# Flamingo-style four-layer block: the causal attention of the second layer in two halves of the tokens, the first one beside the gather

## The chip, the cores and the metric

The kernel runs on one core of a Trainium2 chip. A core has TensorE (PE, with its weight loads as PEld), VectorE (DVE), ScalarE (ACT), GpSimd (POOL) and SyncE (SP), and 16 DMA engines. The metric is device time in microseconds, median of the runs; the time before is 6575.31 us (three runs, 6571.84 to 6575.43).

## The reference

There are 2048 tokens of width 256 and a context of M = 1601 rows. Each of four layers (0 to 3) adds a gated attention to x and then a gated feed-forward. What matters here is this order and layer 2's attention:

```python
x = x + tanh(g_xattn[0]) * _L0_xattn_ref(ctx, ctx, layernorm(x), ...)   # sampled: 80 gathered rows a token
x = x + tanh(g_ffn[0])   * _L0_ffn_ref(layernorm(x), ...)               # with a convolution over tokens, width 3
x = x + tanh(g_xattn[1]) * _L1_xattn_ref(layernorm(x), ctx, ctx, ...)   # all 1601 keys
x = x + tanh(g_ffn[1])   * _L1_ffn_ref(layernorm(x), ...)
x = x + tanh(g_xattn[2]) * _L2_xattn_ref(layernorm(x), ctx, ctx, ...)   # causal
x = x + tanh(g_ffn[2])   * _L2_ffn_ref(layernorm(x), ...)               # experts, over all tokens
...
# _L2_xattn_ref: 16 heads of 16
q, k, v = query @ Wq.T, key @ Wk.T, value @ Wv.T
causal = arange(sq)[:, None] >= arange(sk)[None, :]     # token i sees context rows 0..i, of the 1601
out = softmax(where(causal, q k^T * SCALE, NEG)) v;  out @ Wo.T
```

A token of layers 1 and 2 needs nothing of the tokens after it, and of the tokens before it only what the convolution of layer 0 takes from its neighbour.

## The kernel before, in words

**Tokens and stages.** Tokens are in NT = 16 tiles of 128. `ALL_STAGES` places stages one after the other. Between two stages every engine that takes part waits for the others to be done (`run`). A stage placed with `skip=("pool",)` and others "beside" it lets POOL work on its own stage while PE, ACT, DVE and SP go through the stages beside.

**The gather.** `stage_gather_late` is POOL's: for each of the 7 last token tiles it issues 80 indirect DMAs (`gather`, L1319), each of which brings one row a partition from a table in memory to `got_late`, and then stores the tile (2.56 MB) to `late_rows` (L1391). Beside it stand three stages for tokens 0 to 1023: the convolution feed-forward of layer 0, the attention of layer 1 and the gated feed-forward of layer 1. `stage_sample_late` comes after both and loads `late_rows` (L1412, first loads L1224 and L1225); it computes the layer 0 attention of the last 7 tiles. Then come the same three stages for tokens 1024 to 2047, then the attention of layer 2 for all tokens, then the experts.

**An attention stage** (`stage_attention(env, keep, scratch, n, t0, nt)`, tokens of tiles t0 to t0+nt):

- Start: layer norm, the query projection in float32, split into bfloat16 parts and stored to `q_parts` (24 DMAs, L372).
- Heads in 8 pairs; hh is 0 or 1 in a pair. For each head there are two passes over the scores. The maximum pass ("max") multiplies queries by keys with tokens as rows (L657, causal diagonal L660) and reduces on DVE (L789); its "row" step (L795, L797) makes the negated maxima, which SP stores and loads back as one more row of `q_exp` (L877, L879). The exponential pass ("score") multiplies with keys as rows (L675, diagonal L678), ACT takes exp (L745), and the "sum" step multiplies the result by the values in float32 (L694), four groups of T/4 tokens side by side on the array. DVE copies the sums out at the end of a head (L802), SP stores them in 8 DMAs (`store_sums`, L885 and L887).
- The order is written out ahead: `exp_timeline` and `max_timeline` give each step a due time from costs, and the sorted list is the order in which PE, and with it DVE, work. `max_only` holds the maxima of the first pair, `both` is the loop's body (the exponential steps of a pair and maxima of the next, 7 times), `exp_last` the last pair. ROW_LEAD = 12 puts the maxima of a head 12 us ahead of its exponentials.
- SP's loop is, for each pair and each hh: `load_exp` (L868, L869: waits until the scores of the same hh of the pair before are through), `load_row` (L877 four times, waits for the row and for the store, then L879), `load_max` of the next pair (L861, L862), `store_sums` of the pair before (waits for the store at its end).
- End: the denominators go through memory (L917 to L940), DVE multiplies by their inverse (L814), PE projects (L721), DVE adds to X (L832).

For layer 2 a query tile t sees min(1601, 128(t+1)) keys, a key tile t is seen from token 128t on.

Of the kernel before, what the change touches and what calls it, by code (L numbers as in the profile page):

```python
# [16 lines left out]
P = 128  # L17
S = 2048
D = 256
DC = D // P  # L20
NT = S // P
# [4 lines left out]
M = 1601  # L26
MT = (M + P - 1) // P
# [458 lines left out]
def stage_attention(env, keep, scratch, n, t0, nt):  # L486
# [10 lines left out]
    tag = f"a{n}_{t0}"  # L497
    own = n == 3
    causal = n == 2
    keys = M + S if own else M  # L500
    KT = MT + (NT if own else 0)
    PE_CH, PE_SUM, ACT_FIXED, ACT_CH = 0.22, 0.92, 0.5, 0.37
    ROW_LEAD = 12.0
    SUM_LAG = 1.0
# [3 lines left out]
    def sb(name, shape, dt=f32, where=scratch):  # L508
        return where.enter_context(nc.sbuf_tensor(f"{tag}_{name}", shape, dt))

    def sem(name):
        return env.sem(f"{tag}_{name}")


    tiles = [(P * t, min(P, M - P * t), P * t if causal else 0, causal) for t in range(MT)]
    if own:
        tiles += [(M + P * t, P, P * t, True) for t in range(NT)]

# [1 line left out]
    exp_units = []  # L520
    order = [(hh, t) for hh in range(2) for t in range(KT)]
    for hh, t in order:
        for c in range(tiles[t][2] // CH, chunks):
            exp_units.append((hh, t, c, max(tiles[t][2], CH * c)))
    unit_of = {(hh, t, c): i for i, (hh, t, c, _) in enumerate(exp_units)}
    last_chunk_tile = {c: max(t for t in range(KT) if tiles[t][2] < SUM * (c + 1)) for c in range(4)}

    max_units, max_steps = [], []
    for hh in range(2):
        for t in range(nt):  # L530
            seen = M + P * (t + 1) if own else (min(M, P * (t + 1)) if causal else M)
            d0 = M + P * t if own else P * t
            d1 = min(d0 + P, seen) if (own or causal) else d0
            for k0 in range(0, seen, MAX_COLS):
                max_steps.append(("max", len(max_units)))
                max_units.append((hh, t, k0, min(MAX_COLS, seen - k0), d0, d1))
        max_steps.append(("row", hh))
# [3 lines left out]
    def exp_timeline(hh):  # L541


        out, now = [], 0.0
        for t in range(KT):
            units = [i for i, u in enumerate(exp_units) if u[0:2] == (hh, t)]
# [32 lines left out]
    wq, wo = sb("wq", [P, DC, D]), sb("wo", [P, DC, D])  # L579
    values = sb("values", [P, KT, D])  # L580
    q_bias = sb("q_bias", [P, DC])
# [13 lines left out]
    probs = [sb(f"probs{k}", [P, CH]) for k in range(PROB_SLOTS)]  # L595
    v_head = [sb(f"v_head{k}", [P, KT, 32]) for k in range(2)]
    sums = [sb(f"sums{k}", [P, SUM]) for k in range(2)]
# [8 lines left out]
    w_in, qb_ready, self_v, self_out = sem("w_in"), sem("qb_ready"), sem("self_v"), sem("self_out")  # L606
# [144 lines left out]
    def vector(dve):  # L751
# [31 lines left out]
        def steps(x, what, last=False):  # L783
            for s in what:
# [13 lines left out]
                elif s[0] == "out":  # L798
                    hh = s[1]
                    dve.wait_ge(sums_done, x * NS_ + (KT * (hh + 1) + NS_))  # L800
                    dve.wait_ge(sums_free, x * 2 + hh + 1)
# [36 lines left out]
    def sync(sp):  # L838
# [6 lines left out]
        if own:  # L845
            sp.dma_start(wk[:, :, :], dram["wk3"].rearrange("(c p) e -> p c e", p=P)).then_inc(w_in, 16)
            sp.dma_start(wv[:, :, :], dram["wv3"].rearrange("(c p) e -> p c e", p=P)).then_inc(w_in, 16)
        sp.dma_start(values[:, 0:MT, :], env.v_rows[n]).then_inc(w_in, 16)
        if n == 1:
            any_masked = sp.value_load(mask["flag"][0:1, 0:1])  # L850
            with sp.If(any_masked > 0):
# [472 lines left out]
def sample_buffers(env, keep):  # L1324

    def sb(name, shape, dt=env.f32):
        return keep.enter_context(env.nc.sbuf_tensor(name, shape, dt))
    env.Q0, env.frac, env.rows = sb("queries", [P, NT, D]), sb("frac", [P, NT, NO]), sb("rows", [P, NT + 1, NO], env.i32)
    env.got_late = sb("got_late", [P, NO, 4 * HD])
    env.numbers = sb("numbers", [P, NO], env.i32)  # L1330
# [834 lines left out]
def build(nc, dram):  # L2165
# [3 lines left out]
    with ExitStack() as keep:  # L2169
# [15 lines left out]
        def place(make, *args, hold=None, skip=(), beside=()):  # L2185
# [3 lines left out]
            with ExitStack() as scratch:  # L2189
# [4 lines left out]
                append(emitters, (), own)  # L2194

        ALL_STAGES(env, place, keep)
        block = keep.enter_context(nc.Block())

# [40 lines left out]
def ALL_STAGES(env, place, keep):  # L2239
    from contextlib import ExitStack  # L2240
    half = NT // 2
    place(stage_prep)
    env.any_masked = keep.enter_context(env.nc.sbuf_tensor("any_masked", [1, 1], env.i32))
    with ExitStack() as sampling:
        sample_buffers(env, sampling)
        with ExitStack() as front:
            place(stage_ctx, hold=front)
            place(stage_sample_points, hold=front)
            place(stage_sample_early, skip=("pool",), beside=(
                (stage_kv, (1,), True), (stage_quant,), (stage_fill,), (stage_mask_flag,),  # L2250
                (stage_sample_first,), (stage_kv, (2, 3), False)))
        place(stage_gather_late, skip=("pool",), beside=(
            (stage_conv_ffn, 0, half), (stage_attention, 1, 0, half), (stage_gated_ffn, 0, half)))
        place(stage_sample_late)
    place(stage_conv_ffn, half, half)
    place(stage_attention, 1, half, half)
    place(stage_gated_ffn, half, half)
    place(stage_attention, 2, 0, NT)
    place(stage_expert_ffn, 2)
    place(stage_attention, 3, 0, NT)  # L2260
    place(stage_expert_ffn, 3)
    place(stage_store)
# [68 lines left out]
```

## Time and profile before

| | us |
|---|---|
| median of 3 runs | 6575.31 |
| lowest, highest | 6571.84, 6575.43 |
| span of the profiled execution | 5943.9 |
| PE busy (of the span) | 3795.9 (64%) |
| DVE busy | 2791.6 (47%) |
| ACT busy | 1990.8 (33%) |
| POOL busy | 1506.2 (25%) |
| mean granted TensorE clock | 0.791 |
| layer 2 attention, from L839 to the last L832 | 2834.2 to 3488.2 |

The span runs from the first to the last instruction of one profiled execution; the page gives no time of that execution from outside, and the median lies 631.4 us over the span. Busy times are sums over the whole span; the stages have different limits, so a change in one stage is read from that stage. The granted clock is 1.00 at 2.4 GHz and 0.50 at 1.2 GHz.

### The profile page before, as it was taken

To read this page: it belongs to the slowest core of one execution; us is meant where nothing else is said; L and a number is where in the kernel's file an instruction comes from. 1 tells how busy PE (TensorE), PEld (TensorE's weight loads), DVE (VectorE), ACT (ScalarE), POOL (GpSimd) and SP (SyncE) were. 2 spreads that over 40 slices of the span, in tenths; PEclk is the share of its full clock that TensorE was granted. 3 is DMA by queue.
4 is the path that set the end of the run, shared out by engine and by line. 5 is a ranking of instruction groups with operands and counts; after the bars stand their busy time and mean duration, and the time that the engine had idled before them with its cause. 6 is when DMAs were issued, how large, how long until landed. Compare 5 with 4: busy or idle time off the path is not lost.

```text
span 5943.9 us, 71309 instructions
## 1 busy us (share of the span) xinstructions
PE 3795.9 (64%) x19888; PEld 1731.9 (29%) x19894; DVE 2791.6 (47%) x3817; ACT 1990.8 (33%) x3720; POOL 1506.2 (25%) x1461
## 2 busy tenths in 40 slices
PE   7700410037962013996599969974899999997695
PEld 2300200022321001332133336862222222222485
DVE  3131221276753276776566630013766666673201
ACT  1100100014751001673155621212366666664131
POOL 0767777677767400000000010010000000000202
PEclk9555655557986555998699979986799999999698
DMA  2331311013321211110211111534100111101243
GB/s 83 90 118 24 108 38 24 21 55 106 92 93 39 92 66 48 51 51 20 81 52 47 42 60 65 192 137 117 43 25 25 32 33 33 33 25 32 110 181 135
DMA packets 195461, 403.88 MB, mean 68 GB/s; under 512 B 46405, under 2 KB 130649, under 8 KB 186074
## 3 DMA queue, kind: packets, MB, share of 16 engines
q1 hardware_dynamic: 147114, 323.79, 17.0%
q0 software_dynamic: 48112, 77.16, 4.6%
q8 instruction: 122, 2.00, 0.1%
q14 instruction: 113, 0.93, 0.1%
HBM read 301.77 MB, written 106.10 MB: 69 GB/s over the span
## 4 chain that ended last, share of the span: by engine, by line
PE 47%; POOL 20%; DVE 10%; issue 10%; DMA 7%; ACT 2%; SPq 1%; POOLq 1%; DVEq 1%; ACTq 0%; PEldq 0%
POOL got_late L1319 13%; PE PS L694 13%; PE PS L657 9%; PE PS L675 8%; POOL s_got L1319 6%; PE PS L1959 5%; PE PS L1969 5%; DVE a_maxima L789 3%; ACT a_probs L745 1%; DMA q_parts<-a_parts 1%; PE PS L1929 1%; DMA late_rows<-got_late 1%; PE PS L1937 1%; PE PS L1122 1%; DMA Y<-denominators 1%
## 5 line engine op out<-in xcount | busy, mean ns | idle before, releaser
L789 DVE TENSOR_REDUCE a_maxima<-PS 128x1 f32<-128x1024 f32 (+8 forms) x1696 | 1637.9, 990 | 685.3 <-PE PS L657 468.7
L745 ACT ACTIVATE a_probs<-PS 128x512 f32<-128x512 f32 (+4 forms) x2896 | 1503.3, 572 | 771.7 <-PE PS L675 568.3
L657 PE MATMUL PS<-a_k_max,a_q_max 96*128 96x512 bf16 (+2 forms) x3136 | 913.5, 371 | 153.1 <-DVE a_maxima L789 90.4
L675 PE MATMUL PS<-a_q_exp,a_k_exp 97*128 97x512 bf16 (+4 forms) x2896 | 970.2, 376 | 58.6 <-ACT a_probs L745 30.6
L694 PE MATMUL PS<-a_probs,a_v_head 128*32 128x256 f32 (+4 forms) x7456 | 964.5, 496 | 31.8 <-DVE a_v_head L804 11.2
L2145 POOL IOTA e_slot_no<- 128x23 f32 x2 | 0.3, 162 | 2944.1 <-DVEq L2207 2944.1
L1319 POOL DMA_INDIRECT got_late<-kv_table,numbers x560 | 576.8, 1030 | 171.9 <-issue 171.9
L675 PEld LDWEIGHTS PS<-a_q_exp,a_k_exp 97*128 97x128 bf16 (+1 forms) x2896 | 271.7, 99 | 697.6 <-ACT a_probs L745 442.7
L657 PEld LDWEIGHTS PS<-a_k_max,a_q_max 96*128 96x128 bf16 x3136 | 263.8, 100 | 692.9 <-DVE a_maxima L789 386.6
L1319 POOL DMA_INDIRECT s_got<-kv_table,s_numbers x400 | 428.5, 1071 | 121.9 <-issue 121.9
L1298 PE MATMUL PS<-identity,s_ctx 128*128 128x128 f32 x18 | 6.2, 449 | 668.9 <-DVE s_ctx L1274 668.9
L1319 POOL DMA_INDIRECT got_late<-kv_table,s_numbers x320 | 348.5, 1089 | 96.9 <-issue 96.9
L1959 PE MATMUL PS<-e_slotT,e_w 128*128 128x256 f32 x1280 | 287.2, 383 | 11.7 <-DMA e_w<-in_ew 11.7
L2011 ACT ACTIVATE e_hid<-PS,e_w 128x256 f32<-128x256 f32 x320 | 151.4, 473 | 409.2 <-PE PS L1959 409.2
L694 PEld LDWEIGHTS PS<-a_probs,a_v_head 128*32 128x32 f32 (+1 forms) x7456 | 169.3, 108 | 407.9 <-ACT a_probs L745 241.8
L1969 PE MATMUL PS<-e_w,e_hid 128*128 128x256 f32 x1280 | 283.0, 379 | 1.4 <-ACT e_hid L2011 1.4
L1959 PEld LDWEIGHTS PS<-e_slotT,e_w 128*128 128x128 f32 x1280 | 246.1, 192 | 46.4 <-issue 12.3
L1969 PEld LDWEIGHTS PS<-e_w,e_hid 128*128 128x128 f32 x1280 | 240.2, 190 | 33.1 <-issue 2.2
L2158 POOL DMA_INDIRECT e_got<-slots_out,e_place_i x64 | 64.0, 999 | 711.3 <-SPq L1893 692.4
L1287 ACT ACTIVATE s_weight<-s_score 128x80 f32<-128x80 f32 x9 | 2.4, 269 | 634.9 <-DVE s_score L1266 634.9
L1298 PE MATMUL PS<-identity,m_ctx 128*128 128x128 f32 x14 | 4.8, 447 | 326.4 <-DVE m_ctx L1274 326.4
L1298 PEld LDWEIGHTS PS<-identity,s_ctx 128*128 128x128 f32 x18 | 2.6, 204 | 674.4 <-DVE s_ctx L1274 674.4
(342 smaller groups left out, 3309.9 us busy)
## 6 DMA issues: line engine op xcount, KB each, us to landing
e_w<-in_ew SPq DMA_DIRECT2D x41, 2052.0 KB, 8.1
late_rows<-got_late POOLq DMA_DIRECT2D x7, 2560.0 KB, 7.9
m_got<-late_rows SPq DMA_DIRECT2D x7, 2560.0 KB, 9.2
a_k_max<-k_parts SPq DMA_DIRECT2D x48, 300.2 KB, 3.8
a_k_exp<-k_parts SPq DMA_DIRECT2D x48, 300.2 KB
a_q_max<-q_parts SPq DMA_DIRECT2D x32, 384.0 KB, 3.6
a_q_exp<-q_parts SPq DMA_DIRECT2D x32, 384.0 KB
a_k_max<-k_parts SPq DMA_DIRECT2D x16, 684.2 KB, 5.7
```

The source lines that it names most:

```text
L657: last = pe.matmul(bank[:, b0:b1], q_max[hh][:, P * t:P * (t + 1)], k_max[hh][:, k0 + b0:k0 + b1], start=True, stop=not (lo < hi or masked))
L675: last = pe.matmul(bank[0:rows, q - CH * c:CH], k_exp[hh][:, k0:k0 + rows], q_exp[hh][:, q:CH * (c + 1)], start=True, stop=not (on_diag or ...
L694: last = pe.matmul(sum_bank[32 * c:32 * c + 32, q - SUM * c:SUM], v_head[hh][0:rows, t, :], probs[i % PROB_SLOTS][0:rows, q - at:SUM * (c ...
L745: act.activation(probs[i % PROB_SLOTS][0:rows, q - CH * c:CH], exp_bank[i % EXP_BANKS][0:rows, q - CH * c:CH], ACT.Exp).then_inc(probs_rea ...
L789: dve.tensor_reduce(maxima[hh][:, t, k0 // MAX_COLS:k0 // MAX_COLS + 1], max_bank[s[1] % MAX_SLOTS][:, 0:w], AX.X, ALU.max).then_inc(max_t ...
L1122: pe.matmul(bank, env.CT[:, c, c0:c0 + P], wkv[:, c, :], start=(c == 0), stop=False)
L1319: pool.indirect_dma_start(out=got[:, j, :], out_offset=None, in_=env.table, in_offset=bass.IndirectOffsetOnAxis(ap=numbers[:, j:j + 1].bit ...
L1929: last = pe.matmul(PS[:, f % 4, :], w1[1][:, c, P * f:P * (f + 1)], env.YT[:, c, CH * chunk:CH * (chunk + 1)], start=(c == 0), stop=(c == ...
L1959: last = pe.matmul(PS[:, f % 4, 0:SLOT], w1[k][:, c, P * f:P * (f + 1)], slotT[k][:, c, :], start=(c == 0), stop=(c == DC - 1))
L1969: last = pe.matmul(PS[:, 4 + k, D * j:D * (j + 1)], hid[k][:, f, P * j:P * (j + 1)], w2[k][:, f, :], start=(f == 0), stop=(f == FT - 1))
L2011: act.activation(hid[k][:, f, 0:SLOT], PS[:, f % 4, 0:SLOT], ACT.Gelu_apprx_tanh, bias=b1[k][:, f:f + 1]).then_inc(hid_out, 1)
L2158: pool.indirect_dma_start(out=got[t % FETCH][:, k, :], out_offset=None, in_=env.slots_out, in_offset=bass.IndirectOffsetOnAxis(ap=place_i[ ...
```

## The change

The causal attention takes a first token tile t0 that is not 0 and a number of tiles that is not 16, and it is placed twice: tiles 0 to 7 as a fourth stage beside the gather, tiles 8 to 15 where the whole was. Key tiles are cut to those that the half can see (`CT`: 8 of 13 for the first half, 13 for the second); in the second half the key tiles below t0 are seen by all of its tokens and have no diagonal. The value rows that are loaded are cut in the same way.

```diff
@@ stage_attention
-    keys = M + S if own else M
-    KT = MT + (NT if own else 0)
+    keys = M + S if own else (min(M, P * (t0 + nt)) if causal else M)
+    CT = (keys + P - 1) // P if causal else MT
+    KT = CT + (NT if own else 0)
...
-    tiles = [(P * t, min(P, M - P * t), P * t if causal else 0, causal) for t in range(MT)]
+    tiles = [(P * t, min(P, M - P * t), max(0, P * (t - t0)) if causal else 0, causal and t >= t0) for t in range(CT)]
...
-            seen = M + P * (t + 1) if own else (min(M, P * (t + 1)) if causal else M)
-            d0 = M + P * t if own else P * t
+            seen = M + P * (t + 1) if own else (min(M, P * (t0 + t + 1)) if causal else M)
+            d0 = M + P * t if own else P * (t0 + t)
...
-        sp.dma_start(values[:, 0:MT, :], env.v_rows[n]).then_inc(w_in, 16)
+        sp.dma_start(values[:, 0:CT, :], env.v_rows[n][:, 0:CT, :]).then_inc(w_in, 16)
@@ ALL_STAGES
         place(stage_gather_late, skip=("pool",), beside=(
-            (stage_conv_ffn, 0, half), (stage_attention, 1, 0, half), (stage_gated_ffn, 0, half)))
+            (stage_conv_ffn, 0, half), (stage_attention, 1, 0, half), (stage_gated_ffn, 0, half),
+            (stage_attention, 2, 0, half)))
         place(stage_sample_late)
...
     place(stage_gated_ffn, half, half)
-    place(stage_attention, 2, 0, NT)
+    place(stage_attention, 2, half, half)
```

## Rows read from the trace of the kernel before

**Rows 1.** Busy time by stretch (start:end length, PE, PEld, DVE, ACT, POOL, PEclk, DMA, GB/s).
```profile
1843.30:2021.50 178.20, 0.00 (x0) 0.00 (x0) 0.00 (x0) 0.00 (x0) 122.08 (x125) 0.50 0.16 52
1430.00:1700.00 270.00, 254.81 (x2065) 86.67 (x2064) 211.65 (x264) 192.01 (x339) 187.48 (x193) 1.00 0.32 95
2450.00:2695.00 245.00, 230.94 (x1870) 78.28 (x1869) 191.72 (x239) 173.22 (x306) 0.00 (x0) 1.00 0.16 51
2985.00:3410.00 425.00, 407.71 (x2369) 129.52 (x2372) 288.17 (x375) 251.80 (x503) 0.00 (x0) 1.00 0.17 46
2371.00:2391.00 20.00, 12.67 (x34) 3.22 (x34) 16.61 (x20) 0.00 (x0) 0.00 (x0) 0.50 0.15 48
4380.00:4390.00 10.00, 6.87 (x22) 1.86 (x23) 2.58 (x3) 4.43 (x7) 0.00 (x0) 0.50 0.25 62
4391.00:4401.00 10.00, 9.19 (x53) 2.66 (x51) 7.11 (x9) 7.12 (x13) 0.00 (x0) 1.00 0.00 1
```

**Rows 2.** Chain of waits, 1836 to 2045 us (start, length, what), and one piece near 4378.
```profile
2013.59 7.80 DMA late_rows<-got_late
2021.56 6.69 POOLq L2207
4378.29 4.66 issue
```

**Rows 3.** Waits, 1836 to 2035 us (who waited for whom: total, times, longest).
```profile
DVE m_bo L1238 <- DMA m_bo<-in_bo: 191.6, 1, 191.6
```

**Rows 4.** Timeline, first and last instructions of stages (start, length, engine, line).
```profile
1315.26 0.39 SPq L839 DMA_DIRECT2D a_wq<-in_wq  x1
1371.35 1.03 PE L657 MATMUL PS<-a_k_max,a_q_max 96*128 96x512 bf16 x2 [17.74 <-DMA a_k_max<-k_parts]
1841.51 0.48 DVE L1767 SCALAR_TENSOR_TENSOR X<-PS,g_worth,X 128x256 f32<-128x256 f32 x1 [3.74 <-PE PS L1692]
2028.51 0.40 SPq L1224 DMA_DIRECT2D m_wo<-in_wo  x1
2310.94 0.38 SPq L839 DMA_DIRECT2D a_wq<-in_wq  x1
2726.04 0.41 DVE L802 COPY a_sums<-PS 128x256 f32<-128x256 f32 x1
2749.85 0.48 DVE L832 SCALAR_TENSOR_TENSOR X<-PS,a_keep_q,X 128x256 f32<-128x256 f32 x1 [0.38 <-PE PS L721]
2834.24 0.40 SPq L839 DMA_DIRECT2D a_wq<-in_wq  x1
2916.39 0.74 DVE L789 TENSOR_REDUCE a_maxima<-PS 128x1 f32<-128x128 f32 x2 [12.46 <-PE PS L660]
2920.81 3.64 DVE L789 TENSOR_REDUCE a_maxima<-PS 128x1 f32<-128x896 f32 x4 [0.20 <-PE PS L660]
3487.69 0.48 DVE L832 SCALAR_TENSOR_TENSOR X<-PS,a_keep_q,X 128x256 f32<-128x256 f32 x1 [0.38 <-PE PS L721]
```

**Rows 5.** Timeline, DVE's copies of hh = 0's and 1's sums, layers 1 and 2.
```profile
2459.96 0.41 DVE L802 COPY a_sums<-PS 128x256 f32<-128x256 f32 x1
2671.06 0.41 DVE L802 COPY a_sums<-PS 128x256 f32<-128x256 f32 x1
3113.43 0.69 DVE L802 COPY a_sums<-PS 128x512 f32<-128x512 f32 x1 [0.64 <-PE PS L694]
3176.84 0.69 DVE L802 COPY a_sums<-PS 128x512 f32<-128x512 f32 x1 [0.64 <-PE PS L694]
```

**Rows 6.** Timeline of SP's DMA issues for one head, layer 1.
```profile
1516.87 1.71 SPq L877 DMA_DIRECT2D neg_max<-a_neg_t  x4
1519.75 0.25 SPq L879 DMA_DIRECT2D a_q_exp<-neg_max  x1
...
1526.97 0.34 SPq L869 DMA_DIRECT2D a_k_exp<-k_parts  x1
```

**Rows 7.** DMA issues of the page (size each, us to landing).
```profile
a_k_max<-k_parts SPq DMA_DIRECT2D x48, 300.2 KB, 3.8
```

## The prediction

> **What bounds the kernel now.** I read busy time by stretch first, because the span's averages mix stages. From 1843.3 to 2021.5 us PE, DVE and ACT run nothing and POOL is busy for 122 of 178 us [rows 1]: the three stages beside the gather are through at 1842.0 (1841.51 + 0.48), and the sampling of the last tiles starts at 2028.5 [rows 4]. The chain of waits says what holds them: POOL's last store (2013.59 + 7.80) and 6.69 us until POOL has handed over [rows 2]. DVE waits 191.6 us in one piece for the first load that follows [rows 3]. So there is a hole of 2028.5 - 1842.0 = 186.5 us in which only the gather works. Outside it the gather bounds nothing.
>
> The layer 2 attention takes 2834.2 to 3488.2, 654.0 us [rows 4]. In its loop PE is busy 407.7 of 425 us at a granted clock of 1.00 (2.4 GHz), in layer 1's 230.9 of 245 [rows 1]. Both are bound by PE. A pair of heads takes 63.4 us in layer 2 (3176.84 - 3113.43) and 42.2 us in a half of layer 1 ((2671.06 - 2459.96) / 5) [rows 5].
>
> **What the change removes, adds and moves.** No score is computed twice or left out: per head 4608 columns (first half, 8 key tiles) and 12032 (second, 13 tiles) make the 16640 of before in the exponential pass, 4608 + 11780 = 16388 in the maximum pass. What is new is a second start and a second end, SP's 17 DMAs a head twice, and 21 sum steps of 256 columns a head for 13 of 512. The whole first half moves ahead of the sampling, onto PE, ACT, DVE and SP, and past nothing on POOL's queue, where it issues nothing.
>
> *Second half.* Its shape is that of layer 1 on 8 tiles with all keys, which took 2310.94 to 2750.33, 439.4 us [rows 4]. Columns of a head: 12032 for 13312 in the exponential pass, 11780 for 12808 in the maximum pass, 2308 fewer, 0.96 us at 2.4 GHz; against them stand ten diagonal products of 128 columns, 0.53 us, and as many more steps. So the loop stays at 42 us a pair. The 16 maximum units ahead of the loop and ACT's tail lose a few us, and the bias of layer 1 falls away: 435 us, between 430 and 441.
>
> *First half, PE.* A head has 9216 columns of scores, 16 diagonals of 128 (2048), together 4.7 us at 2.4 GHz, and 8 sum steps. A float32 sum goes at four cycles a column: layer 1's head is 26120 columns (10.9 us) and 13 steps of 256 (5.55 us), 16.4 us of the 21.1 measured [rows 5], and the remaining 4.7 us over its 71 steps are 0.066 us each. The same on layer 2's whole head gives 26.2 us of columns, 31.7 measured, 0.047 us for each of 116 steps. So the first half's head takes 4.7 + 3.2 for the sums + 48 steps at 0.047 to 0.066: 10.2 to 11.1 us, I take 10.6, a pair 21.2. At 1.2 GHz the 7.9 us of columns double: 17.
>
> *First half, SP.* From L877 to the end of L869 there are 1526.97 + 0.34 - 1516.87 = 10.4 us when nothing is waited for but the two stores [rows 6]; with the hop to the next L877 10.6 us a head. That is 21.2 a pair, as much as PE. In the stages of before this chain had 21 or 32 us for a head and hid; now nothing hides it. From the issue of L868 to the landed keys of L862 there are about 8.9 us: 1 for the two loads, 4 up to the end of L862's issue and 3.8 to land [rows 6, 7]. In steady state these run under the other head's 10.6, with 2 us to spare. Two equal bounds rarely meet exactly and the gather's transfers run beside, so I take 23 us a pair, with 21.2 and 26 as ends.
>
> *First half, the sum.* It starts at 1843.3, SP's 1.3 us after the last X. Start until the first maximum product: 55, from 1315.26 to 1371.35, 56.1 us, which stands beside the gather with one more load [rows 4]. Maxima of pair 0, all on PE at 0.50 as in the stretch 2371 to 2391 [rows 1]: layer 2's first eight units take about 7 us (2916.0 to 2922.9, halfway through the four in the second row) [rows 4], two heads 14, and the keys for pair 1 land at 15. The first head of the loop runs at 1.2 GHz: 17. Then six periods: 6 x 23 = 138. From the last L868 of hh = 0: SP's two heads 20.6, the round through memory of the first denominators, which in layer 1 hid below 15 us of exponentials, another 16: 37 until the last copy of sums. The close, from 2726.04 to 2750.33, 24 us [rows 4]. Together 55 + 15 + 17 + 138 + 37 + 24 = 286 us, so it ends at 2129.3, and the sampling starts at 2130.6 instead of 2028.5: 102 us late. The gather is through at 2028 in any case and no longer decides.
>
> *In all:* 102 + 435 - 654 = -117 us. That is against the profiled execution, whose span is 5943.9 us; the median lies 631.4 above it, of which I let nothing change: 6575.3 - 117 = **6458 us**. Of the 186.5 us of the hole the change fills all, and gives 70 back: a second start and end (about 80 us) less what the shorter sum steps save.
>
> The gather itself isn't slowed by work beside it: 193 POOL instructions in 270 us beside the attention of layer 1, 1.40 us each, 125 in 178.2 us, 1.43 each, in the hole [rows 1]. Should the DVE's and ACT's new work cost it 20 us, nothing is lost, as the first half is longer than it by 100. The rest of the kernel (sampling, second half's feed-forwards, experts) runs as before, only earlier or later.
>
> **The rivals.**
>
> *Cold clock in the first half.* PE waits for SP's chain at each head, the clock goes to 1.2 GHz and a head takes 17 us, a pair 34. The price is 6 x 11 + 6 = 72 us: 6530. For it: the stretch of maxima alone, PE busy 12.7 of 20 us, stood at 0.50, and one pause of 4.66 us in layer 3's loop [rows 2] put the next 10 us at 0.50, then the clock came back [rows 1]. Against it: the first half keeps PE at about 21 of 23 us, like the loops that held 1.00, and at 1.2 GHz it would be busy without a break, which is what has brought the clock back in each loop.
>
> The Trainium skill, TensorE: Matmul & The Clock Gate, section "HAM oscillation — how this bites in real kernels", says that a loop whose products are shorter than its wait for DMA has the clock taken back in every round. By that rule the time would be the 6530 of this rival. The trace agrees on the pause of 4.66 us; whether the first half has such pauses no row shows.
>
> *The heads' chains don't overlap.* If PE can't start a head before SP's round for it, and SP not before PE has finished the other, a pair costs 2 x (8.9 + 17) = 52 us, at 1.2 GHz as PE idles a third. The first half then takes 286 + 6 x 29 + 15 = 475 us and the change ends slower: +72, 6647. This decides from 403 us on, a pair of 42.5. For it: q_exp and k_exp have one buffer for each hh. Against it: L868 waits only for the same hh of the pair before, and in both loops of before SP was ahead by half a period.
>
> *The hole isn't used.* If the first half were held until the gather is through, it would stand in the open: 287 + 435 - 654 = +68, 6643. Against it: the attention of layer 1, placed in the same way, ran at 1315 beside the gather [rows 1, 4].
>
> **How the numbers follow.** The forecast 80 in 100, its own range 6436 (floor of 21.2 us a pair, short starts, second half 430) to 6489 (26 a pair, second half 441); cold clock 13; no overlap 4; hole not used 3. The range 6436 to 6512 leaves out most of the cold case and both slow ones and takes in a clock that is cold for part of the time. About 0.2% (13 us) is what can be told from no change here. Faster 0.93, within 0.01, slower 0.06.
>
> **What would show it.** Right: the last L832 of the first half near 2129, L1224 at 2131 instead of 2028.5; copies of L802 for one hh 21 to 26 us apart, SP without waits for rows; clock near 1.00 from the second pair on; second half 430 to 441 us with copies 42 us apart; the gather's last store still near 2014. Wrong: copies more than 28 us apart, a clock of 0.50 in the loop, a start after 2021, or a second half above 450.

## The result, and the profile after

| | median us | lowest to highest | runs |
|---|---|---|---|
| before | 6575.37 | 6571.84 to 6577.65 | 4 |
| after | 6627.23 | 6618.69 to 6634.47 | 4 |

The ratio is 1.008, interval 1.0069 to 1.0092: the change costs 52 us. The forecast was 6458, a gain of 117.

One thing is needed to read every number below. The same program runs at one of two levels, and all runs of a batch, made together on one chip, lie at the same one: the kernel before took 5953 and 5959 us (medians) in two batches of the experiments and 6572 to 6589 in four, with nothing measured between. The six batches ran on six chips, so whether the level belongs to the chip or to the hour can't be told. I call them the low and the high level. The medians above are of the high level; the profile that the prediction used (span 5943.9) is of a run at the low one. In every run of the experiments the time is only some 2 us above the span of its profile (5952.35 and 5950.6, 6618.69 and 6616.9). So the 631.4 us that the prediction let lie outside the span were inside the span of the runs that were timed.

The page of the kernel after, at the high level (busy time, then tenths in 40 slices, then the chain by engine):

```profile
span 6616.9 us, 74701 instructions
PE 3844.4 (58%) x20918; PEld 1764.1 (27%) x20918; DVE 2809.7 (42%) x3921; ACT 2015.9 (30%) x3742; POOL 1483.1 (22%) x1461
...
PE   6240121001222495741597598799389999998496
...
POOL 1715764767676300000000000100100000000101
...
PE 46%; issue 15%; DVE 11%; another core or an unknown queue 9%; DMA 6%; POOL 4%; SPq 4%; ACT 3%; DVEq 1%; POOLq 0%; ACTq 0%
```

In the slices in which POOL gathers PE stands mostly at 0 to 2 tenths, though four stages of work are placed beside the late tiles' gather. The timeline's marks of the kernel after, in order: the gather's last store, the end of layer 1's first half, start and end of layer 2's first half, the sampling, start and end of layer 2's second half.

```profile
2230.66 0.58 POOL L1392 DMA_DIRECT2D late_rows<-got_late  x1 [2.10 <-DMA got_late<-kv_table,numbers]
...
2553.60 0.48 DVE L833 SCALAR_TENSOR_TENSOR X<-PS,a_keep_q,X 128x256 f32<-128x256 f32 x1 [0.38 <-PE PS L722]
2636.82 0.40 SPq L840 DMA_DIRECT2D a_wq<-in_wq  x1
2905.49 0.48 DVE L833 SCALAR_TENSOR_TENSOR X<-PS,a_keep_q,X 128x256 f32<-128x256 f32 x1 [0.38 <-PE PS L722]
2908.53 0.39 SPq L1225 DMA_DIRECT2D m_wo<-in_wo  x1
3712.61 0.40 SPq L840 DMA_DIRECT2D a_wq<-in_wq  x1
4147.97 0.48 DVE L833 SCALAR_TENSOR_TENSOR X<-PS,a_keep_q,X 128x256 f32<-128x256 f32 x1 [0.38 <-PE PS L722]
```

The first half starts 406 us *after* the last store. What it should have stood beside was over. The kernel before at this level is e10 (below); its marks are the gather's last store, the end of layer 1's first half, the sampling, and start and end of layer 2:

```profile
2232.34 0.58 POOL L1391 DMA_DIRECT2D late_rows<-got_late  x1 [2.08 <-DMA got_late<-kv_table,numbers]
2558.71 0.48 DVE L832 SCALAR_TENSOR_TENSOR X<-PS,a_keep_q,X 128x256 f32<-128x256 f32 x1 [0.38 <-PE PS L721]
2643.03 0.40 SPq L1224 DMA_DIRECT2D m_wo<-in_wo  x1
3449.21 0.40 SPq L839 DMA_DIRECT2D a_wq<-in_wq  x1
4102.29 0.48 DVE L832 SCALAR_TENSOR_TENSOR X<-PS,a_keep_q,X 128x256 f32<-128x256 f32 x1 [0.38 <-PE PS L721]
```

Here the sampling follows the stages beside the gather at once, and the gather has been over for 411 us: the hole of [rows 1, 3, 4] isn't there. The sum with these marks: the sampling starts 2908.5 - 2643.0 = 265.5 us late, layer 2 takes 4148.5 - 3712.6 = 435.9 for 4102.8 - 3449.2 = 653.6 us, 217.7 less. Net +47.8; the two spans differ by 44.4 (6616.9 and 6572.5, from two batches), the medians of the result by 52.

Against the low level (e1: the convolution feed-forward of the first half, short conv, starts at 1191.4, the sampling at 2028.1) the kernel before loses 229 us up to the conv (1420.3), 386 more up to the sampling, and 7 in all that follows. So the 622 us between the levels lie where POOL gathers: the gather of the early tiles, then that of the late ones. How they are lost, between 1660 and 2240 us of the kernel after (windows as in [rows 1], its second line just after the gather):

```profile
1660.00:2240.00 580.00, 114.69 (x436) 32.98 (x436) 80.92 (x131) 45.10 (x80) 405.43 (x413) 0.52 0.22 63
2240.00:2400.00 160.00, 152.55 (x1222) 51.33 (x1214) 123.25 (x150) 111.60 (x199) 0.00 (x0) 0.99 0.16 47
```

PE has 436 products in 580 us while POOL gathers, and 1222 in the next 160 us, within the same stage. Waits there (who, for whom: total, times, longest):

```profile
DVE a_maxima L790 <- remote: 281.5, 25, 33.5
...
ACT a_probs L746 <- remote: 243.8, 18, 24.7
...
PE PS L676 <- ACT a_probs L746: 141.3, 11, 22.5
```

"remote" and "another core or an unknown queue", on a single core, mean here that the signal which ended the wait has no record. A piece of the timeline shows one such round:

```profile
1816.09 0.76 DVE L790 TENSOR_REDUCE a_maxima<-PS 128x1 f32<-128x577 f32 x1 [4.36 <-remote]
...
1816.91 0.66 PE L658 MATMUL PS<-a_k_max,a_q_max 96*128 96x512 bf16 x2 [4.09 <-issue]
...
1821.69 1.22 DVE L790 TENSOR_REDUCE a_maxima<-PS 128x1 f32<-128x1024 f32 x1 [4.84 <-issue]
```

PE's two products take 0.66 us together and are through at 1817.57, yet DVE, which has nothing else to do, reads them at 1821.69, 4.1 us later. SP is late even on instructions that touch no other engine, the loop of L372 beside the early gather (min/median/max ns of one; first the kernel after at the high level, then at the low):

```profile
L372 SPq MOVE k_parts<-kv_parts x24: 14/700/1395, 159.2 to 271.8; - x24
```

```profile
L372 SPq MOVE k_parts<-kv_parts x24: 29/39/39, 160.9 to 199.7; - x24
```

This is not so on every engine. From 150 to 1190 us of the kernel after, 151 of SP's 198 register and branch instructions and 94 of POOL's 591 take over 300 ns, and none of the 448 of PE, ACT and DVE; in e7 none on any engine.

### The profile page after: what moved, and what is told of

Same layout as the page of the kernel before. It is cut to its first block, busy times and chain, and to the rows that moved or that the text cites. A ratio compares the mean times of both kernels' runs of the same rounds, so it can differ in the third digit from the quotient of the medians.

```text
span 6616.9 us, 74701 instructions
## 1 busy us (share of the span) xinstructions
PE 3844.4 (58%) x20918; PEld 1764.1 (27%) x20918; DVE 2809.7 (42%) x3921; ACT 2015.9 (30%) x3742; POOL 1483.1 (22%) x1461
## 4 chain that ended last, share of the span: by engine, by line
PE 46%; issue 15%; DVE 11%; another core or an unknown queue 9%; DMA 6%; POOL 4%; SPq 4%; ACT 3%; DVEq 1%; POOLq 0%; ACTq 0%
PE PS L695 12%; PE PS L658 9%; PE PS L676 8%; PE PS L1960 4%; PE PS L1970 4%; DVE a_maxima L790 3%; SPq L372 2%; POOL s_got L1320 2%; ACT a_probs L746 2%; POOL got_late L1320 1%; DMA q_parts<-a_parts 1%; DMA Y<-denominators 1%; PE PS L1938 1%; PE PS L1930 1%
## 5 line engine op out<-in xcount | busy, mean ns | idle before, releaser
L790 DVE TENSOR_REDUCE a_maxima<-PS 128x1 f32<-128x1024 f32 (+9 forms) x1696 | 1639.2, 991 | 1045.8 <-PE PS L658 491.3
L676 PE MATMUL PS<-a_q_exp,a_k_exp 97*128 97x512 bf16 (+4 forms) x2896 | 988.9, 380 | 204.4 <-ACT a_probs L746 176.4
L658 PE MATMUL PS<-a_k_max,a_q_max 96*128 96x512 bf16 (+3 forms) x3136 | 927.1, 375 | 308.6 <-DVE a_maxima L790 135.0
L1320 POOL DMA_INDIRECT got_late<-kv_table,s_numbers x320 | 333.9, 1044 | 96.8 <-issue 96.8
L695 PEld LDWEIGHTS PS<-a_probs,a_v_head 128*32 128x32 f32 (+1 forms) x8448 | 189.8, 109 | 540.3 <-issue 284.8
L326 PE MATMUL PS<-CT,kv_wk 128*128 x96 | 67.3, 861 | 202.2 <-issue 144.4
```

The lines of the kernel that those rows point to most:

```text
L326: last = pe.matmul(env.PS[:, k, 0:width], weight[:, c, P * half:P * (half + 1)], source[:, c, bass_ds(chunk * width + first, width)], star ...
L658: last = pe.matmul(bank[:, b0:b1], q_max[hh][:, P * t:P * (t + 1)], k_max[hh][:, k0 + b0:k0 + b1], start=True, stop=not (lo < hi or masked))
L676: last = pe.matmul(bank[0:rows, q - CH * c:CH], k_exp[hh][:, k0:k0 + rows], q_exp[hh][:, q:CH * (c + 1)], start=True, stop=not (on_diag or ...
L695: last = pe.matmul(sum_bank[32 * c:32 * c + 32, q - SUM * c:SUM], v_head[hh][0:rows, t, :], probs[i % PROB_SLOTS][0:rows, q - at:SUM * (c ...
L790: dve.tensor_reduce(maxima[hh][:, t, k0 // MAX_COLS:k0 // MAX_COLS + 1], max_bank[s[1] % MAX_SLOTS][:, 0:w], AX.X, ALU.max).then_inc(max_t ...
L1320: pool.indirect_dma_start(out=got[:, j, :], out_offset=None, in_=env.table, in_offset=bass.IndirectOffsetOnAxis(ap=numbers[:, j:j + 1].bit ...
```

## The experiments

"Before" is always the kernel before, run beside the kernel named. Batches: e1 to e4 low, e5 high, e6 to e8 low, e9 and e10, e11 and e12, e13 to e15 high.

**The kernel before once more (e1), nothing edited.**

> The kernel before, unchanged, for a second profile. Theory A (beside the gather the signals between engines are late, in the timed runs of both kernels; the profile of before that the prediction used was of an execution without this): its span is near 6570 us, the stages beside the gather end after the gather's last store, and there is no hole of 186 us. Theory B (the hole is there in the timed runs too and the 631 us lie outside the span): the span is near 5944 us again, hole included.

Measured: 5952.35 us, before 5959.1 (5952.29 to 5962.81). This batch lay at the low level. The span and the hole are theory B's, but the 631 us that it puts outside the span are not there: time and span are 1.8 us apart. So neither theory came as written. The hole is there as in the prediction's profile:

```profile
1842.00:2028.00 186.00, 0.00 (x0) 0.00 (x0) 0.00 (x0) 0.00 (x0) 122.52 (x126) 0.50 0.17 50
```

**The split without the move (e2).**

```
-            (stage_gated_ffn, 0, half), (stage_attention, 2, 0, half)))
+            (stage_gated_ffn, 0, half)))
...
+    place(stage_attention, 2, 0, half)
     place(stage_attention, 2, half, half)
```

> The layer 2 attention in two halves, both after the gated feed-forward of the second half, none beside the gather. Theory A: only the cost of the second start and end, +35 us over before (250 + 437 - 654 from the stages of the changed kernel's profile): 6610 us. Moving the half beside the gather then adds the rest, to 6627. Theory B (the first half beside the gather disturbs the gather or is disturbed by it, the split itself is cheap): within 10 us of before, 6575 to 6585.

Measured, at the low level: 6007.18 (6002.97 to 6011.5), before 5959.1, ratio 1.008 (1.0063 to 1.0097), +48 us, more than the +35 and the 10 that were expected. First half 2840.2 to 3108.0, 268 us, second 3110.7 to 3547.9, 437. Two halves take 268 + 3 + 437 = 708 for 654: in the open the split costs about 50 us. That it costs as much at the high level is read from the marks above: there the halves take 269 and 436 for 654.

**The gather with nothing beside it (e3).**

```
-        place(stage_gather_late, skip=("pool",), beside=(...))
+        place(stage_gather_late)
+        place(stage_conv_ffn, 0, half)
+        place(stage_attention, 1, 0, half)
+        place(stage_gated_ffn, 0, half)
```

> The kernel before with the gather of the last 7 tiles as a stage of its own, the three stages that stood beside it after it. Without late signals this must cost the whole overlap: the three stages take 650 us (1192 to 1842 in the profile that the prediction used), so 6575 + 650 - 187 = 7038 us or more. Theory A (late signals beside the gather make the three stages outlast it): gather 830, stages 650, against some 1150 together, +330: about 6905 us, and the three stages take 650 again in its profile.

Measured: 6581.31, before 5959.1. The overlap is worth 622 us at the low level. As a difference that is more than the +463 of the first expectation (650 - 187): all three stages now stand after the gather, and the sampling starts at 2657.6 instead of 2028.1, so the hole should not have been taken off. As it happens it is also the time of the high level, but by another road: here layer 1's first half ran 2135.0 to 2572.7, 438 us, after the gather. The equal times are no proof of anything; layer 1's first half alone has 1659.7 to 2553.6, 894 us, in the result.

**The change without the late tiles' indirect DMAs (e4, e8).**

```
-            gather(env, pool, env.got_late, env.numbers, gathered)
-            pool.wait_ge(gathered, j * (16 * NO) + 16 * NO)
```

> The changed kernel without the 560 indirect DMAs of the late gather (the rows of the last 7 tiles are then not the right ones); stores stay. Theory A: the four stages beside run at full speed: 650 + 250 us, and 6627 falls by about 400 to 500 us (what the late signals cost between 1420 and 2240), to near 6180. Theory B: nothing was held by the gather's traffic, so at most the few us of shared DMA go, 6600 or more.

> The changed kernel without the 560 indirect DMAs of the late gather (the rows of the last 7 tiles are then not the right ones), at this call's level. At the low level 5817 as in e4. At the high level theory A says that only stretches beside a gather are late: the early gather's (150 to 1420) stays stretched by some 230 us, the four stages of the late one run as in e4: near 6045.

Measured: 5817.13 and 5815.51 (before 5959.1 and 5952.91), both at the low level, as the second text has it; the 6180 and 6600 of the first were for the high one and stay open. First half 1838.5 to 2108.5, 270 us. Beside e7's 5828.62 the gather costs the change 11 to 13 us: it is hidden, as forecast.

**The change once more (e5).**

> The changed kernel, unchanged, timed beside the kernel before. In e1 the kernel before took 5952 us with the span of the profile that the prediction used; in the runs of the result it took 6575. Theory C (the change itself works as forecast where the signals between engines aren't late; the +52 us is what it does where they are late): if before comes out near 5955 here, the change is faster by 130 to 140 us, 5818, as the first half takes 270 us from 1838 and the second 435 (e4), and the sampling starts at 2111 instead of 2028. If before comes out near 6575, the change is +52 again. Theory D (the first half beside the real gather brings the late signals on, whatever the chip): before near 5955 and the change at 6600 or more.

Measured: 6644.99 (6640.37 to 6646.21), before 6589.02, ratio 1.0084 (1.0067 to 1.0101). The result repeats (+56 us), and this batch lay at the high level. It left open whether the change makes a run slow or the level does.

**Before and after in one batch (e6, e7).**

> The kernel before again, for a profile beside the change on one chip. Two levels of the same kernel have been seen, 5959 us (e1) and 6589 us (beside e5). If it is at 6580 here: theory A says that its stages beside the gather are stretched (the attention of layer 1 ends after the gather's last store, the sampling starts near 2650 instead of 2028) while everything after is as in e1. If it is at 5955, no news but the pair for e7.

> The changed kernel once more. Theory C (the level belongs to the chip or the session, the change gains where signals are in time): at a level of 5955 for before 5818, at 6580 for before 6635. Theory D (the first half beside the real gather brings late signals on): 6600 or more whatever before does.

Measured: e6 5954.33, e7 **5828.62** (5825.69 to 5830.17), before 5952.91, ratio 0.979 (0.9773 to 0.9806): **-124 us at the low level**. That the change brings the high level about is out: both kernels have both. Marks of e7, in the order of those above:

```profile
1850.65 0.40 SPq L840 DMA_DIRECT2D a_wq<-in_wq  x1
...
2017.63 0.58 POOL L1392 DMA_DIRECT2D late_rows<-got_late  x1 [3.02 <-DMA got_late<-kv_table,numbers]
...
2125.02 0.48 DVE L833 SCALAR_TENSOR_TENSOR X<-PS,a_keep_q,X 128x256 f32<-128x256 f32 x1 [0.38 <-PE PS L722]
2128.07 0.39 SPq L1225 DMA_DIRECT2D m_wo<-in_wo  x1
...
2936.34 0.40 SPq L840 DMA_DIRECT2D a_wq<-in_wq  x1
...
3367.62 0.48 DVE L833 SCALAR_TENSOR_TENSOR X<-PS,a_keep_q,X 128x256 f32<-128x256 f32 x1 [0.38 <-PE PS L722]
```

Its windows (same columns), layer 1's first half, the loop of layer 2's first half, and the stretch that stands above for the high level:

```profile
1317.00:1766.00 449.00, 362.89 (x2672) 129.15 (x2672) 294.80 (x402) 250.19 (x446) 318.70 (x325) 0.87 0.34 96
1932.00:2045.00 113.00, 102.37 (x803) 40.12 (x802) 67.34 (x120) 63.40 (x126) 63.98 (x65) 1.00 0.39 117
1660.00:2240.00 580.00, 332.77 (x2212) 140.50 (x2208) 334.38 (x528) 189.62 (x353) 250.73 (x249) 0.76 0.32 101
```

**The kernel before without the late tiles' indirect DMAs, high level (e9), and with nothing edited (e10).** e9's edit is that of e4.

> The kernel before without the 560 indirect DMAs of the late gather (the rows of the last 7 tiles are then not the right ones). It takes the hole away at whatever level: the stages beside then end after the gather. Theory E (the change is worth the hole and costs the split; where there is no hole it is slower by the split's price): 5953 - 187 = 5766 us, so the changed kernel without the gather (5816 in e4 and e8) is slower than this by 50 us, the +52 of the result. Rival F (the +52 comes from the first half being stretched beside the gather): then without the gather the change costs nothing or gains, and this is at 5816 or above.

> The kernel before for a profile at the high level, should this call have it (6580): the attention of layer 1 for tokens 0 to 1023 ends near 2550, 310 us after the gather's last store near 2240; the sampling starts near 2640. At the low level 5953 and nothing new.

Measured: e9 5995.8 (5993.62 to 5997.97), before 6571.55, ratio 0.9123 (0.9097 to 0.915); e10 6574.26. In e9 layer 1's first half ran 1542.0 to 1980.5, 438.5 us, as fast as anywhere, with 228 us lost before it, beside the early tiles' gather that was left in (conv at 1419.4). So at the high level only what stands beside indirect DMAs is slow. The expected 5766 left out those 228 us; with them it is 5994. The comparison with the changed kernel (theory E against rival F) wants both without the gather at one level, and the changed one ran so at the low level only: 5995.8 - 228 = 5768 is 48 us under e4 and e8, which speaks for E as an estimate.

e10 is the profile of before shown above, with 2559 and 2643 for the expected 2550 and 2640. It also shows the lateness beside a third place with indirect DMAs, the experts after layer 2 (32 of them, 4161.7 to 4201.6): ACT waits 3.75, 4.21 and 7.71 us before the third to fifth of its activations, where it waited 1.03 in the profile that the prediction used, and DVE's first L2109, which adds the shared expert's result to X, starts 54.7 us after the first of these DMAs instead of 43.9.

**POOL pauses after so many indirect DMAs until they have landed (e11, e12 on the change, e13 on the kernel before, e15 on the change).** GROUP is 8, 4, 8 and 16, for early and late tiles.

```
 for j in ...:
+    if j and j % GROUP == 0:
+        col = j // GROUP - 1
+        pool.wait_ge(arrived, before + 16 * j)
+        pool.tensor_tensor(env.pace[:, col:col + 1], numbers[:, 0:1],
+                           numbers[:, 0:1], env.ALU.add).then_inc(env.paced, 1)
```

> The changed kernel with a pause after each 8 indirect DMAs of both gathers, until they have landed (9 pauses of some 2.3 us for 80 DMAs, a tile at 137 instead of 116 us). Theory G (the late signals are a backlog that the gather's DMAs build up faster than it drains, so a slower gather ends it): at the high level (before 6575) the stages beside run as at the low one, the gather ends near 2360, the total near 6065. Rival H (whatever is late stays late as long as POOL gathers): at the high level later than 6630 by the 330 us of the pauses, near 6900. At the low level both say 5828 + 240 = 6065.

> The same with a pause after each 4: 19 pauses, a tile at 160 us, the gather ends near 2720. Low level: near 6430. High level: by theory G also near 6430, by rival H near 7300.

> The kernel before with the pauses of e11. Its four stages less one: at the high level the attention of layer 1 then ends near 2233 and the gated part near 2316 as in e11, the gather at 2389, so a hole of 70 us is back. Theory E with G (the change is worth the hole that there is, less the split's 50): 6312 - 215 (sampling at 2395 instead of 2604 is -209) + 218 (one layer 2 stage of 654 for 436) = 6320, within 15 us of e11. Rival H (the change is slower by 50 at the high level whatever the gather does): 6260. At the low level: gather to 2360 in the open, 5953 + 330 = 6285, and e11's kernel there 6065.

> The changed kernel with a pause after each 16: 4 pauses for 80 DMAs, a tile at 125 us. Theory G (a backlog, drained in pauses): between e11 and no pauses at the high level, 6312 < t < 6627, near 6450. Rival I (the pauses matter only in that any one wait resets what is late, their number doesn't): as e11 or better, 6250 to 6310. At the low level 5940.

Measured:

| | median us | before, in its batch | ratio (interval) | layer 1's first half | last store |
|---|---|---|---|---|---|
| e11, 8 | 6312.25 | 6575.83 | 0.9598 (0.957 to 0.9626) | 711 us | 2381.2 |
| e12, 4 | 6459.73 | 6575.83 | one run | 543 us | 2734.3 |
| e13, before, 8 | 6314.34 | 6582.26 | 0.9589 (0.9561 to 0.9616) | 723 us | 2358.6 |
| e15, 16 | 6564.23 | 6582.26 | 0.9984 (0.9946 to 1.0022) | 931 us | 2284.5 |

A pause of about 1.5 us after each 8 takes 268 us off the kernel before (e13, in one batch). The changed kernel comes out 264 us under the kernel before (e11); its own time without pauses was 6627 and 6645 in other batches, so it gains 315 to 333 by these. In e11, the stretch of layer 1's first half and one pause:

```profile
1522.00:2233.00 711.00, 471.74 (x2672) 141.46 (x2672) 294.82 (x401) 251.52 (x446) 422.63 (x467) 0.73 0.25 73
...
1701.42 0.19 POOL L1324 TENSOR_TENSOR pace<-numbers 128x1 int32<-128x1 int32 x1 [1.52 <-DMA got_late<-kv_table,numbers]
1702.11 1.00 POOL L1325 DMA_INDIRECT got_late<-kv_table,numbers  x1 [0.50 <-issue]
```

These are the same 2672 products as in e7's 449 us. So neither theory of e11 is right: its 6312 lies between the 6065 of G, by which all lateness ends, and the 6900 of H. The early tiles' gather (conv at 1397.6) and the conv beside the late one (124 us, as in e7) are free of it, layer 1's attention is not. Pauses after 4 make the stages beside the late tiles' gather faster still, but the gather of the early tiles takes 198 us longer (conv at 1595.3 for 1397.6), and the late one bounds the sampling (2749.2, 79 us after layer 2's first half). As the gather itself bounds it, that e12 is near G's 6430 says little for G. So 4 pays for the late tiles alone, which is e14.

Pauses after 16 bring the changed kernel level with the kernel before (0.9984 for 1.008 and 1.0084 without them), some 60 to 80 us less by other batches. That is inside the bounds of theory G, 115 us above its 6450, and rules out rival I. The trace shows why 16 does so much less than 8. In the five profiles of the high level in which POOL issues at least 16 in a row (after, e5, e9, e10, e15), the first of SP's register instructions to take over 300 ns starts after the ninth or tenth indirect DMA, 11.5 to 13.3 us after the first. In e15 they are then slow until the pause that ends at 175.6, quick again until 188, and slow again. With a pause after each 8, 4 of 198 between 150 and 1190 us are slow in e11, against 151 in the kernel after and none in e7. So the lateness sets in after some nine DMAs without a pause. This isn't all of it: from 1420 to 2230 us, beside the late tiles, 44 of SP's 542 are still slow in e11.

With both kernels at 8 there is no difference between them (6312 and 6314, expected 6320 for e13): in e11 the first half stands after the last store in part again (2318.2 to 2601.0), and in e13 the hole is back, but 48 us long (2325.4 to 2373.5).

**Pauses after 8 in the early tiles, 4 in the late ones, on the change (e14).**

> The changed kernel with a pause after each 8 in the early gather and each 4 in the late one. In e11 the early gather was through at 1397 without late signals, in e12 the late one kept its neighbours to 1074 us instead of 1203. Theory G, both together: late gather 1397 + 1145 = 2545, the four stages 1397 + 1074 = 2471, sampling at 2557 instead of 2604: 6312 - 47 = 6265. At the low level 6230, slower than e11 there.

Measured: **6261.91** (6261.71 to 6262.12), before 6582.26, ratio 0.9509 (0.9481 to 0.9537). Layer 2's first half runs 2156.9 to 2482.6, all of it before the last store at 2530.6. The forecast of 6265 held. It is 320 us under the kernel before in its batch and some 365 under the changed kernel (6627, another batch). It wasn't run at the low level. An estimate from rows: its sampling starts at 2545.5, and the rest of e7 after its sampling takes 5827.2 - 2128.1 = 3699 us, so about 6245 there if the gather takes as long, above the 5953 of the kernel before. By this estimate it is a remedy for the high level alone.

## Why the prediction was wrong

**The hole** (the prediction's first part, and "the median lies 631.4 above it, of which I let nothing change") is the step that failed. The hole of 186.5 us was read from a run at the low level and applied to a median of the high one. There the stages placed beside the gather keep the sampling back until 411 us after it, so the term of +102 for the first half is +266: nothing of it is hidden. The term -219 for layer 2 (435 - 654) measured -218. A tenth of the median lay outside the profile, and I took it for something that the kernel has outside its span; no row said so, and every run here has 2 us there.

**The rivals.** The nearest in size is "the hole isn't used", +68 for +52, with a chance of 3 in 100. Its mechanism is not what happened: the first half wasn't held back by the gather, it came when the gather was long over. Of the cold clock: at the low level the loop kept 1.00, so that rival fell there. The heads' chains overlapped (next point).

**The mechanism, where the hole exists,** came out in the main as worked out, in e7:

- In all -124 us for -117, from 5953.
- First half 1850.65 to 2125.5, 275 us for 286; sampling at 2128.1 for 2130.6; second half 432 for 435. That the sampling is so near is in part luck: the first half started 7 us later than forecast and took 11 less (82 us up to the first copy of sums for 87, 135 for the 138 of six periods, 58 for 61 after).
- A pair takes 22.2 us for 23 (five of the six periods; the other takes 24.0). Here the reading of what sets it was off: the forecast had PE and SP equal at 21.2. PE needs 22.2 with its own waits. From 1932.8 to 2021.7, four pairs of 22.2 us each, it is busy 81.8 of 88.9 us, waits for exponentials and maxima and for no DMA, while SP waits for its two stores only and never for PE:

```profile
PE PS L676 <- ACT a_probs L746: 4.0, 4, 1.0
PE PS L658 <- DVE a_maxima L790: 1.5, 4, 0.4
...
PEld PS L676 <- ACT a_probs L746: 16.2, 32, 1.2
...
SPq L880 <- DMA neg_max<-a_neg_t: 11.6, 8, 2.0
SPq L891 <- DMA denominators<-a_sums: 7.7, 8, 1.1
```

  SP is back at L878 after 10.7 to 11.7 us (10.6 predicted), so it falls behind a little with each pair. In the fifth, at the gather's last store, four of its issues take 4.86 us instead of 1.71 and its round 14.6; there PE waits for the keys, once, and the period is 24.0:

```profile
1998.58 1.71 SPq L878 DMA_DIRECT2D neg_max<-a_neg_t  x4
2009.59 1.71 SPq L878 DMA_DIRECT2D neg_max<-a_neg_t  x4
2021.14 4.86 SPq L878 DMA_DIRECT2D neg_max<-a_neg_t  x4
2032.04 0.23 PE L658 MATMUL PS<-a_k_max,a_q_max 96*128 96x128 bf16 x1 [2.06 <-DMA a_k_max<-k_parts]
```

- The gather kept its pace: last store 2017.63 for "near 2014". That work beside it costs it nothing is not quite so: from the first to the last of the late tiles' DMAs it takes 797 us with nothing beside it (e3), 817 beside three stages (e1) and 820 beside four (e7).

**The clock.** Two products of 512 columns start 0.40 us apart at 1816.9 in the kernel after, where the granted clock is 0.50 (1.2 GHz), and 0.22 apart in e7's loop at 1.00 (2.4 GHz). Beside the gather at the high level the granted clock was 0.52 with PE busy 115 of 580 us, 0.99 just after it; at the low level it was 1.00 with PE busy 102.4 of 113. The Trainium skill, TensorE: Matmul & The Clock Gate, section "HAM oscillation — how this bites in real kernels", tells of a clock that is taken back in each round of a loop that waits longer than it multiplies. The trace agrees, though the waits here are for late signals and not for loads. It is a consequence here and a small part: from the conv to the sampling PE is busy 473.7 us in e10 and 433.9 in e1, with the same products. That is 40 us of the 386 lost.

**What is shown and what isn't.** Shown: the level is a matter of the batch and not of the kernel (e1, e5, e6, e7, e10); what is late stands beside indirect DMAs alone (e9, and the windows on both sides of 2240); pauses of POOL take part of it away (e11 to e14), after 16 only a little (e15). Not shown: what makes a batch high or low, and what it is in the chip that the indirect DMAs keep busy. That signals are late is a reading of waits that end long after the work they wait for. Nor is it shown that recording has no part in it: every timed run here was recorded too, and records are missing in just these traces.

## What to carry to other kernels

Before anything is worked out from a profile, its span belongs beside the median: where they are 10% apart, the profile may be, as here, of another kind of execution, and its holes may not exist in the runs that are timed. A stage that is to fill a hole needs the hole's two ends at that level, and here it takes the open price of the split (50 us) against the hidden one (-124). Where indirect DMAs run beside other work, look at short instructions on idle engines in that stretch; if they are late, pausing after each 8 DMAs, or 4 where the gather has time to spare, can be worth more than a new order of the stages (-268 us here), and by the estimate above costs time where nothing is late.

## What the runs showed of the hardware

- Beside a run of indirect DMAs, one each 1.3 us on POOL's queue, signals between the other engines came late in some batches: DVE waited 4.4 to 4.8 us around two products of 0.66 us, up to 33.5 us in one piece, and SP's register instructions took 700 ns (median) for 39, ACT's not. After the last of them PE went from 436 products in 580 us to 1222 in 160 us.
- It sets in after the ninth or tenth indirect DMA in a row, 11.5 to 13.3 us after the first (five profiles), and runs of 32 are long enough for it (e10).
- POOL's own issue of the late tiles isn't late: from the start of the conv to its last store it takes 812 us at the high level (e10) and 822 to 825 at the low (e1, e7).
- With a pause of 1.5 us after each 8 the median of SP's register instructions beside the early tiles' gather was back at 39 ns, while layer 1's first half beside the late tiles' still took 711 us for 449; with 4 it took 543. The loop of L372 in e11:

```profile
L372 SPq MOVE k_parts<-kv_parts x24: 3/39/39, 161.8 to 200.5; - x24
```

- At the high level signals are missing from the trace, 24070 recorded landings for 42257 in the same kernel at the low level (e7). A wait put down to another core, in a program on one core, stands in the traces of both kernels at the high level and in none at the low.
